# Attention B of a four-layer block: scores made twice, the second time with keys on the partitions

## What is computed

```python
scores = jnp.einsum('bhqd,bhkd->bhqk', qc, k) * scale
...
scores = jnp.where(causal_mask[None, None], -jnp.inf, scores)
m = jnp.max(scores, axis=-1, keepdims=True)
...
p = jax.nn.softmax(scores - m, axis=-1)
oc = jnp.einsum('bhqk,bhkd->bhqd', p, v)
```

## Time and profile before

| | |
|---|---|
| median of 3 runs | 11101.68 us (11082.91 to 11107.82) |
| the profiled execution, its own time | 11115.23 us |
| its span, first to last instruction | 11113.4 us |
| busy: PE, PEld | 9422.7 us (85%), 6711.5 us (60%) |
| busy: ACT, DVE, POOL | 6687.5 us (60%), 6258.0 us (56%), 2944.3 us (26%) |
| mean granted TensorE clock | 0.947 |
| the four attention B stages | 727, 737, 744 and 737 us |

### The profile page before, as it was taken

The page is one execution under the profiler, slowest core; times in us unless marked ns, Lnnn a source line. Parts: engine busy times, 40 slices in busy tenths (PEclk is TensorE's granted clock), DMA queues, the critical chain, the costliest instruction groups (busy, mean ns, idle before and its releaser), DMA issues. The chain is left out here.

```text
span 11113.4 us, 271423 instructions
## 1 busy us (share of the span) xinstructions
PE 9422.7 (85%) x95520; PEld 6711.5 (60%) x95520; DVE 6258.0 (56%) x14730; ACT 6687.5 (60%) x11009; POOL 2944.3 (26%) x3520
## 2 busy tenths in 40 slices
PE   5888888999688888899968888889996888888999
PEld 3665665666465666566646656656663565665666
DVE  3655663765365566376446556637644565663764
ACT  3666663765466666376546666637644666663764
POOL 2333332001233333200123333310012333331001
PEclk7999999999899999999989999999998999999999
DMA  6999992000699999100069999911007999991100
GB/s 240 378 363 366 381 378 87 26 25 16 233 377 366 361 379 380 59 25 25 16 254 380 367 362 382 365 46 27 23 18 265 373 372 362 379 357 48 27 22 26
DMA packets 747623, 2482.45 MB, mean 223 GB/s; under 512 B 111745, under 2 KB 133761, under 8 KB 745921
## 3 DMA queue, kind: packets, MB, share of 16 engines
q1 hardware_dynamic: 746176, 2463.84, 60.3%
HBM read 1280.34 MB, written 1183.07 MB: 222 GB/s over the span
## 5 line engine op out<-in xcount | busy, mean ns | idle before, releaser
L658 DVE CUSTOM_DVE_ANT_0 z<-sc,z 128x1024 f32<-128x1024 f32 x2048 | 2496.5, 1220 | 1848.5 <-DMA z<-rel_rows 1608.0
L716 POOL TENSOR_SCALAR z<-z,nmax 128x1024 f32<-128x1024 f32 x2048 | 2277.8, 1123 | 4028.5 <-DVE nmax L668 4028.5
L631 ACT ACTIVATE pT<-rg 128x512 f32<-128x512 f32 x4096 | 2445.9, 598 | 738.7 <-PE rg L541 679.5
L541 PE MATMUL rg<-ident,z 128*128 128x128 f32 x16384 | 2527.0, 277 | 77.0 <-issue 68.3
L639 ACT ACTIVATE rel<-rg 128x512 f32<-128x512 f32 x3072 | 1721.1, 596 | 1407.2 <-PE rg L522 1401.8
L541 PEld LDWEIGHTS rg<-ident,z 128*128 128x128 f32 x16384 | 1990.3, 142 | 784.6 <-ACT rel L639 294.4
L522 PE MATMUL rg<-pos_s,qv_s 96*128 96x512 bf16 x4096 | 1590.8, 396 | 1021.4 <-DVE rel L693 901.6
L1013 DVE CUSTOM_DVE_ANT_0 z<-sc,mask 128x1024 f32<-128x1024 f32 (+7 forms) x1536 | 1359.1, 910 | 227.0 <-PE sc L832 173.9
L952 ACT ACTIVATE pT<-rg 128x512 f32<-128x512 f32 (+3 forms) x1792 | 928.4, 550 | 763.0 <-PE rg L885 751.0
L522 PEld LDWEIGHTS rg<-pos_s,qv_s 96*128 96x128 bf16 x4096 | 478.7, 118 | 1498.0 <-DVE rel L693 1150.9
L960 ACT ACTIVATE z<-z,nmax 128x128 f32<-128x128 f32 (+15 forms) x1024 | 1226.6, 1198 | 89.0 <-POOL nmax L978 76.7
(11 more groups left out here) (93 smaller groups left out, 8161.5 us busy)
## 6 DMA issues: line engine op xcount, KB each, us to landing
rel_rows<-rel SPq DMA_DIRECT2D x2048, 512.0 KB, 7.2
z<-rel_rows SPq DMA_DIRECT2D x2048, 512.0 KB, 7.1
xnT<-qu_parts SPq DMA_DIRECT2D x792, 64.0 KB, 2.3
xnT<-v_heads SPq DMA_DIRECT2D x132, 256.0 KB, 4.3
v_heads<-rel SPq DMA_DIRECT2D x8, 4096.0 KB, 12.5
k_sb<-k_parts SPq DMA_DIRECT2D x408, 64.0 KB, 2.3
qv_s<-qv_parts SPq DMA_DIRECT2D x384, 64.0 KB, 6.2
pos_s<-pos_parts SPq DMA_DIRECT2D x384, 64.0 KB, 7.2
```

Source lines behind the costliest of these rows:

```text
L541: mm = e.transpose(rg[:, T_BANK[q], (j - 4 * q) * P:(j - 4 * q + 1) * P], z[:, n % RING, j * P:(j + 1) * P], ident[:, :])
L631: e.activation(pT[:, t % 2, q * CH:(q + 1) * CH], rg[:, T_BANK[q], :], ACT.Exp, scale=SCALE).then_inc(p_ready[q], 1)
L658: e.tensor_tensor_reduce(out=zs, in0=scf[:, 2 * half * CH:2 * (half + 1) * CH], in1=zs, scale=1.0, scalar=-3.0e38, op0=ALU.add, op1=ALU.ma ...
L716: e.tensor_scalar(zs, zs, 1.0, nmax[:, n % 2:n % 2 + 1], ALU.mult, ALU.add).then_inc(AA[done], 1)
```

## The change

Attention B is written anew; the rest keeps its code, apart from small setup (spare zero heads in DRAM are gone). For each head:

- `piece` and `largest`: the scores are made once as before, queries on the partitions, in 24 pieces of up to 1024 columns. The causal mask is now added on PE by a bf16 matmul of 128 columns (`ident_b` by `tri_b`). DVE only takes the negated maximum with `tensor_reduce`; nothing is copied out.
- `split` (POOL), `turn_max` (PE), `copy_max` (ACT), `max_rows` (a DMA): the head's 16 columns of negated maxima are split into three bf16 parts, transposed, and laid down as three more rows of the query operand, against rows of ones in the key operand.
- `scores`: the scores are made a second time with the keys on the partitions: one matmul for each block of 128 keys by up to 512 queries (40 in a head, `BLOCKS`), 99 rows, so that the maximum is subtracted in the product. A mask matmul follows on the 16 diagonal blocks. The banks alternate between two.
- ACT takes exp from PSUM straight to `pT_b`, 40 instructions in a head; it is already the operand that the values matmul needs, so there are no transposes of probabilities and no copies.
- `values`: 40 calls in a head, each with up to four blocks, one for each 32-column group; group t now holds query tile t, so nothing is added up at the end. Four fp32 transposes in a head (`turn_out`) take the place of 16 `combine`s.

The pieces of the next head run in between (`PIECE_STEP`), and the eight shortest of the one after it. A lead-in makes the first head's pieces and maxima, one body of four heads runs three times and a last body once, with heads overlapping from one body to the next. The core of the diff:

```diff
@@ -58,15 +58,29 @@
-LAG = 2
-EARLY = NT // 2 - 1
-B_BANK = [0, 1, 2, 0]
+ST_LEAD = 1
+NG = NT // OB
+BLOCKS = [(g, kb, max(0, kb - OB * g)) for g in range(NG) for kb in range(OB * g + OB)]
+NBLK = len(BLOCKS)
+G_END = [sum(OB * k + OB for k in range(g + 1)) for g in range(NG)]
+OUT_STEP = [G_END[0] + 1, G_END[1] + 1, G_END[2] + 1, NBLK - 1]
+PTS = 8
+EXP_0 = 2
+PIECES = [(t, k0, min(k0 + 2 * CH, (t + 1) * P)) for t in range(NT) for k0 in range(0, (t + 1) * P, 2 * CH)]
+NPC = len(PIECES)
+PC_EARLY = 8
+PIECE_STEP = [[j for j in range(PC_EARLY, NPC) if (j - PC_EARLY) * 26 // 16 == i]
+              + [j for j in range(PC_EARLY) if 29 + j * 11 // 8 == i] for i in range(NBLK)]
+TURN_STEP = 31
+MX_OPS = 7
@@ -166,6 +189,15 @@
+        q_b = [zb[0:KROWS + PARTS, i * S:(i + 1) * S] for i in range(HB)]
+        k_b = [zb[0:KROWS + PARTS, (HB + i) * S:(HB + i + 1) * S] for i in range(HB)]
+        pT_b = pT[:, :, :].rearrange("p r (a c) -> p (r a) c", c=CH)
+        po_b = [op[:, 0:P], rg[:, 2, 0:P]]
+        on_b = [op[:, P:2 * P], rg[:, 2, P:2 * P]]
+        on_b4 = [o.rearrange("p (o w) -> p o w", o=OB) for o in on_b]
+        mx_ps = op[0:PARTS * NT, 2 * P:3 * P]
@@ -806,263 +841,260 @@
+        def in_turn(e, b, lead_in, step):
...
+            with e.Fori(0, 1) as p:
+                lead_in(counts(p))
+            with e.Fori(0, GROUPS - 1) as p:
+                at = counts(p)
+                for n in range(HB):
+                    for i in range(NBLK):
+                        step(p, at, n, i, lambda m: True)
+            with e.Fori(GROUPS - 1, GROUPS) as p:
+                at = counts(p)
+                for n in range(HB):
+                    for i in range(NBLK):
+                        step(p, at, n, i, lambda m: m < HB)
+        def pieces_at(n, i):
+            return [(n + 1 + (j < PC_EARLY), j) for j in PIECE_STEP[i]]
         def pe_attn_b(e, b):
...
+            def piece(at, n, j, fresh):
+                s, k0, k1 = PIECES[j]
+                half, q = j % 2, n * NPC + j
+                if j == 0:
+                    e.wait_ge(BB[f"qk_loaded{n % HB}"], at.pairs + (n // HB + 1) * QK_INC)
+                if not fresh:
+                    e.wait_ge(BB["reduced"], at.pieces + (q - 1))
+                last = k1 == (s + 1) * P
+                for c0 in range(k0, k1, CH):
...
+                                  q_b[n % HB][0:KROWS, s * P:(s + 1) * P], k_b[n % HB][0:KROWS, c0:c1],
...
+                if last:
...
+                    mm = e.matmul(scf[:, edge:edge + P], ident_b[:, :], tri_b[:, :], start=False, stop=True)
+                mm.then_inc(BB["c_ready"], 1)
+            def turn_max(at, n):
+                e.wait_ge(BB["mx_step"], at.steps + (n + 1) * MX_OPS)
+                settle(e)
+                e.transpose(mx_ps, parts_b[:, :, :].rearrange("p a t -> p (a t)"), ident[:, :]).then_inc(BB["mx_turned"], 1)
+            def scores(at, n, i, fresh):
+                g, kb, i0 = BLOCKS[i]
+                if i == 0:
+                    e.wait_ge(BB[f"mx_loaded{n % HB}"], at.rows + 16 * (n // HB + 1))
+                if not fresh:
+                    e.wait_ge(BB["exp_done"], at.blocks + (n * NBLK + i - 1 + EXP_0))
+                bank = rg[:, i % 2, :]
+                mm = e.matmul(bank[:, i0 * P:CH], k_b[n % HB][:, kb * P:(kb + 1) * P],
+                              q_b[n % HB][:, g * CH + i0 * P:(g + 1) * CH], start=True, stop=kb < OB * g)
+                if kb >= OB * g:
+                    mm = e.matmul(bank[:, i0 * P:(i0 + 1) * P], tri_b[:, :], ident_b[:, :], start=False, stop=True)
+                mm.then_inc(BB["s_ready"], 1)
+            def values(at, n, i):
+                g, kb, i0 = BLOCKS[i]
+                if i == 0:
+                    e.wait_ge(BB[f"v_loaded{n % NB}"], at.values + 16 * (n // NB + 1))
+                if kb == 0:
+                    e.wait_ge(BB["out_read"], at.groups + (n * NG + g + 1))
+                e.wait_ge(BB["exp_done"], at.blocks + (n * NBLK + i + 1 + EXP_0))
+                for t in range(i0, OB):
+                    mm = e.matmul(po_b[g % 2][VW * t:VW * (t + 1), :], v_s[n % NB][:, kb, :],
+                                  pT_b[:, i % PTS, t * P:(t + 1) * P], start=kb == 0, stop=kb == OB * g + t)
+                mm.then_inc(BB["pv_done"], 1)
+            def turn_out(at, n, g):
+                e.wait_ge(BB["po_copied"], at.groups + (n * NG + g + 1))
+                e.transpose(on_b[g % 2], po_sb[:, g % 2, :], ident[:, :]).then_inc(BB["out_turned"], 1)
+            def lead_in(at):
+                for j in range(NPC):
+                    piece(at, 0, j, j < 2)
+                turn_max(at, 0)
+                e.wait_ge(BB["ones"], e.snap(b * HB + HB))
+                for j in range(PC_EARLY):
+                    piece(at, 1, j, False)
+                for i in range(ST_LEAD):
+                    scores(at, 0, i, True)
+            def step(p, at, n, i, here):
+                m, k = (n, i + ST_LEAD) if i + ST_LEAD < NBLK else (n + 1, i + ST_LEAD - NBLK)
+                if i == NBLK - 1:
+                    values(at, n, i)
+                if here(m):
+                    scores(at, m, k, False)
+                for h, j in pieces_at(n, i):
+                    if here(h):
+                        piece(at, h, j, False)
+                if i == TURN_STEP and here(n + 1):
+                    e.wait_ge(BB["out_read"], at.groups + (n * NG + NG + 1))
+                    turn_max(at, n + 1)
+                if i < NBLK - 1:
+                    values(at, n, i)
+                for g in range(NG):
+                    if i == OUT_STEP[g]:
+                        turn_out(at, n, g)
+            in_turn(e, b, lead_in, step)
...
         def act_attn_b(e, b):
...
+            def copy_max(at, n):
+                e.wait_ge(BB["mx_turned"], at.heads + (n + 2))
+                e.activation(mrow_b[:, n % 2, :], mx_ps, ACT.Copy).then_inc(BB["mx_copied"], 1)
+            def step(p, at, n, i, here):
+                g, kb, i0 = BLOCKS[i]
+                e.wait_ge(BB["s_ready"], at.blocks + (n * NBLK + i + 1))
+                e.wait_ge(BB["pv_done"], at.blocks + (n * NBLK + i + 1))
+                e.activation(pT_b[:, i % PTS, i0 * P:CH], rg[:, i % 2, i0 * P:CH], ACT.Exp,
+                             scale=SCALE).then_inc(BB["exp_done"], 1)
+                if i == TURN_STEP and here(n + 1):
+                    copy_max(at, n + 1)
+            in_turn(e, b, lambda at: copy_max(at, 0), step)
...
         def dve_attn_b(e, b):
...
+            def largest(at, n, j):
+                s, k0, k1 = PIECES[j]
+                half = j % 2
+                into = mx_b[:, n % 2, s:s + 1] if k0 == 0 else mh_b[:, n % 2, s - NT // 2:s - NT // 2 + 1]
+                e.wait_ge(BB["c_ready"], at.pieces + (n * NPC + j + 1))
+                settle(e)
+                e.tensor_reduce(into, scf[:, 2 * half * CH:2 * half * CH + k1 - k0], AX.X, ALU.max,
+                                negate=True).then_inc(BB["reduced"], 1)
+                if j == NPC - 1:
+                    high = mx_b[:, n % 2, NT // 2:NT]
+                    e.wait_ge(BB["reduced"], at.pieces + (n + 1) * NPC)
+                    e.tensor_tensor(high, high, mh_b[:, n % 2, :], ALU.min).then_inc(BB["mx_step"], 1)
+            def take(at, n, g):
+                e.wait_ge(BB["pv_done"], at.blocks + (n * NBLK + G_END[g] + PTS))
+                e.tensor_copy(po_sb[:, g % 2, :], po_b[g % 2]).then_inc(BB["po_copied"], 1)
+            def normalise(p, at, n, g):
+                done = at.groups + (n * NG + g + 1)
+                e.wait_ge(BB["out_turned"], done)
+                e.reciprocal(rsum[:, :], on_b4[g % 2][:, :, HD]).then_inc(BB["rcp"], 1)
...
+            def step(p, at, n, i, here):
+                for h, j in pieces_at(n, i):
+                    if here(h):
+                        largest(at, h, j)
+                for g in range(NG):
+                    if i == G_END[g] - 1:
+                        take(at, n, g)
+                    if i == OUT_STEP[g]:
+                        normalise(p, at, n, g)
+            in_turn(e, b, lead_in, step)
+        def pool_attn_b(e, b):
+            def split(at, n):
+                top = mx_b[:, n % 2, :]
+                def stepped(k):
+                    e.wait_ge(BB["mx_step"], at.steps + (n * MX_OPS + k))
+                    settle(e)
+                e.wait_ge(BB["mx_turned"], at.heads + (n + 1))
+                stepped(1)
+                e.tensor_copy(half_b[:, 0, :], top).then_inc(BB["mx_step"], 1)
+                stepped(2)
...
+            def lead_in(at):
+                for k in k_b:
+                    e.memset(k[KROWS:KROWS + PARTS, :], 1.0).then_inc(BB["ones"], 1)
+                e.wait_ge(BB["ones"], e.snap(b * HB + HB))
+                settle(e)
+                split(at, 0)
+            def step(p, at, n, i, here):
+                if i == 0 and here(n + 1):
+                    split(at, n + 1)
```

(16 more changed lines are left out.)

290 lines of the change are left out of this document (61 added, 229 removed).

## The result

The changed kernel takes 10738.33 us (median of 4 runs, 10732.28 to 10759.23) against 11104.75 for the kernel before on the same chip (4 runs, 11082.91 to 11111.82): a ratio of 0.9677 (95% interval 0.9658 to 0.9695; that of the two medians is 0.9670). The prediction was 10,800 in a range of 10,610 to 11,010. The profiled execution took 10739.21 us.

The account below looks back on a forecast made before the run. PE was taken as the bound of attention B, 38 us a head against 42.9; 28 + 15 x 38 + 29 + 22 + 9 + 2 = 660 us a stage against 736, 304 less in four, hence 10,800 us (range 10,610 to 11,010).

Parts of the forecast that it names:

- values calls of 0.36: PE in a head: 40 values calls at 0.36 us each, hardly dependent on their 1 to 4 blocks, 14.4 us.
- 0.09 for the entry: PE in a head: 0.09 us for the change to the 32-column form after each of 40 score matmuls, 3.6 us.
- 0.7 at the end of a head: PE at the last fp32 transpose of a head: waits for the copy on DVE and two handshakes, 0.7 us.
- the one for the masks: PE in a head: 32 mask matmuls of 128 columns, taken at 0.08 us each between 0.055 and 0.109, 2.6 us.
- The forecast's 1.05 ns: DVE: all forms from PSUM run near 1.05 ns a column, so the reductions take 22 us in a head.
- The rival of half the rate: DVE becomes the bound: reductions over 2 ns a column, 46 us a head, stage 802, kernel 11,370; chance 0.05.
- 28 forecast: Lead-in of a stage: DVE 22, minimum 0.2, POOL and handshake 2.2, turn and copy 0.7, DMA 0.6 and 2.3; 28 us.
- The DMA 0.6 to issue and 2.3 to land: Lead-in: the DMA of the first head's maxima, 0.6 us to issue and 2.3 to land, its last item.
- 22 + 9 us in a stage: Stage losses: two body restarts at 11 us each, 22, and 9 for a low-clock start and drops in between.
- The forecast's 13 us of half clock: Behind a body restart in the kernel before: clock near half, 0.51, for 13 us while PE did light tiles.
- The rival "the granted clock falls": Attention B at 1.2 GHz: gain gone at a fifth of the stage; at half, 50 us a head, 11,590; chance 0.07.
- The ends of the range: Range of the forecast case: 36 us a head, stage 616, kernel 10,620; 41 us, stage 717, kernel 11,025.

Follow-up runs that it names:

- pairs: The changed kernel with the values calls made two at a time, 20 visits to the 32-column form in a head and not 40: 10444.77 us (0.9401 of before).
- nomask: The changed kernel without attention B's 32 causal mask matmuls in a head, left out for the measurement only: 11393.07 us (1.0288 of before).
- dve: The changed kernel with five of a head's nine 1024-column reductions done twice on DVE: 10896.58 us (0.9806 of before).
- dve_late: The changed kernel with five extra 1024-column reductions on DVE from SBUF in steps 26, 28, 31, 34 and 37 of each head: 11108.37 us (0.9979 of before).
- lead: The changed kernel with four of the lead-in's eight early pieces put ahead of the turn of the maxima: 10748.77 us (0.967 of before).
- warm: The changed kernel with 70 idle PE matmuls ahead of attention B's meeting and 34 more before the first operands: 10776.03 us (0.9688 of before).
- before_hint: The kernel before the change, with a branch hint on the loop of attention B: 11036.52 us (0.9931 of before).
- hint: The changed kernel with a branch hint on the loop that runs attention B's body three times: 10716.32 us (0.9649 of before).
- fours: The changed kernel with four steps' values calls made at a time, 10 visits to the 32-column form in a head: 10451.73 us (0.9407 of before).
- best: The changed kernel with values two at a time, branch hints on the loops of attention A and B, and four early pieces ahead of the turn: 10386.27 us (0.9354).

## Why the prediction was right, and which terms were not

**PE bounds it, and its visits to the 32-column form are the price.** The terms of the head held: values calls of 0.36 whatever their blocks (0.34 to 0.36 measured), 0.09 for the entry (0.10), 0.7 at the end of a head (0.69), exps on ACT and small waits beside it. The Trainium skill, TensorEngine Tiling (Array Packing), Key Properties, says that a change of the tiling mode drains TensorE; it gives no price. The rows agree with it (the 0.10 ahead of the values, the weight loads' waits of 0.2 to 0.4 around them), and pairs measures the price: 20 visits less are 3.7 us, 0.18 for each.

**The head is 36.6 and not 38.** The term that was too high is the one for the masks: 0.08 each was taken, 0.053 measured in nomask (0.038 beside paired values), 0.9 us in a head. The other 0.5 is not placed; it is what several roundings and the 0.2 for small waits can hold.

**DVE.** `tensor_reduce` takes what line 1013 took for the same width: 1.22 us for 1024 columns in both kernels. The forecast's 1.05 ns is what each further column adds; the short forms cost more for each column. So the 22 us in a head were near: the 24 pieces of the lead-in take 26.7 us from 1935.91 on, less ten waits for PE of 0.24 to 1.04, 5.5 together, 21.2. The rival of half the rate is out. The Trainium skill, VectorE: DVE Perf Modes, Rules for kernel authors, advises against `tensor_reduce` on a hot path; here it is as fast as the form it replaced, and between restarts DVE's time costs only where PE's order waits for it (dve, dve_late). In the lead-in it is on the path.

**The lead-in was mis-sized: 28 forecast, 35.7 measured.** "The DMA 0.6 to issue and 2.3 to land" was not what held the first scores: the eight early pieces stood ahead of them in PE's order (lead), 6.3 us where turn, copy and DMA were put at 3.6. And up to the turn it is 29.4 us and not 24.4: the forecast priced the pieces by DVE alone, while DVE waited 5.5 us for PE, which ran at half the clock. The order of the changed kernel had shown the eight pieces. That the half clock is what made DVE wait is argued: warm had the full clock for the first 3 to 5 us only.

**The restarts were near in sum, and the sum is partly luck.** 22 + 9 us in a stage were forecast for two restarts, a start at the low clock and drops in between. The heads with a restart lost 127 us in four stages, 31.7 each, and the first head of a stage 0 to 9.5 us, 2.4 on average: 34. But there were no drops in between, and a restart cost 8.5 to 26.6 us where 11 was put for each. The forecast's 13 us of half clock were read where "PE did light tiles"; before_hint shows that these tiles come with half clock even without the long stand (10.2 us), and hint shows that in the changed kernel, whose pipeline isn't emptied there, seven of eight falls go with the stand. Its length there (13.7 to 54.6 us) was in no term.

**The rival "the granted clock falls" did not come true and was nearer than its 0.07.** The kernel as changed keeps the full clock between restarts. One wait in a head that grows from 0.69 to 1.75 us (dve_late), or 32 small matmuls less (nomask), and the clock is at half for a good part of the stage, and all of the gain is gone. Its argument missed as well: it looked at the 0.2 us gaps in each step, and in the changed kernel each fall inside a stage came with one stand of PE of 3.3 to 3.8 us.

**Arithmetic of the stage.** The lead-in of 35.7, 15 heads of 36.6, 29.6 for the last, 31.7 for restarts and 2.4 for the first head, less 1.7 for two other heads (34.6 before the last, which has fewer pieces, and 36.9 where the last body begins), are 646.7, the measured mean; the forecast was 660. Heads came out 21 us under it and the lead-in 8 over, so the error of 13 is a difference of two larger ones. Without restarts and slow first heads the changed stage would stand near 613. For the kernel before no run shows that: before_hint, at 711, still has the empty pipeline and 10.2 us of half clock at each restart. In heads alone the change is worth 6.3 us each, some 100 in a stage.

**The ends of the range** don't follow from the sum: with heads of 36 and 41 us it gives 630 and 705 us in a stage, not 616 and 717, and so 10,680 and 10,980 for the kernel. The measured time lies inside these as well.

## What to carry to other kernels

Count how often PE changes between the full array and its 32-column form, not the matmuls in that form: here a visit cost 0.18 us beyond its products, and grouping two steps' calls gave 294 us more, four fifths of what the rewrite gave. Group until scores in a row wait for the engine that empties their banks, and no further. Before giving slack on another engine away, look for the one place where PE waits for it: a wait there can cost the clock, many times its own length.

## What was not expected of the hardware

- A stand of PE of 1.75 us inside a busy stretch was followed by half the clock (1.2 GHz), within 2 us, at 15 of the 43 head ends away from restarts that had it (dve_late). Waits of 0.69 us in the same place never were in the changed kernel; in hint one was, with a second stand of 0.52 us close behind it.
- PE then stayed at 1.2 GHz for 3.4 us up to 317 us while it was busy nearly all the time. Behind restarts it was at most 6.8 us with values in pairs and 10.2 in fours or in pairs without masks, 13.7 to 54.6 in the changed kernel, 31 to 317 in nomask. The order is not all of it: lead and warm have the changed kernel's order at the restarts, and there it was 3.4 to 61.4. What brings the clock back was not settled; no run varied the work at half clock by itself.
- Where a loop body started again PE stood for 3.3 to 3.8 us in attention B and 7.8 to 9.4 in attention A. A hint at the top of the body took nearly all of it away in attention B (0.49 left in before_hint), and made PE, ACT or DVE wait 1.2 to 2.9 us some way into the body that follows the loop (hint, best).
